# Perceiver layer on one core: queries and keys made by token and turned, the decay's product through the ring

## The reference, cut to what matters

```python
x = x + cross_attention(layernorm(x), ctx)        # 16 heads of 32: q from x, k and v from ctx
x = x + gated_delta_attention(layernorm(x))       # 16 heads of 32, a recurrence over the tokens
x = x + top2_of_8_experts(layernorm(x))

# in the cross attention
q = x @ q_w + q_b;  kv = ctx @ kv_w + kv_b;  softmax(q k / sqrt(32)) v @ proj_w + proj_b
# in the second layer
q, k, v, gate = x @ Wq.T, x @ Wk.T, x @ Wv.T, x @ Wg.T;  beta = sigmoid(x @ Wb.T)
alpha = exp(-exp(A_log) * softplus(x @ Wa.T + dt_bias))      # one number per token and head
q, k normalised by head;  S = a S;  delta = (v - k S) beta;  S += k delta;  y = q S
```

## Time and profile before

| | us |
|---|---|
| median of 3 runs | 3865.71 (3864.11 to 3868.39) |
| the profiled execution | 3867.77 |
| its span in the profile | 3866.0 |
| TensorE busy, matmuls | 3238.1 (84%) |
| TensorE busy, weight loads | 2369.7 (61%) |
| VectorE busy | 2025.7 (52%) |
| ScalarE busy | 1134.9 (29%) |
| GpSimd busy | 988.6 (26%) |
| mean granted TensorE clock | 0.916 |

### The profile page before, as it was taken

One profiled execution on the slowest core, in us unless ns is written; L12 is line 12 of the kernel. 1 busy time (PEld: TensorE's weight loads), 2 busy tenths in 40 slices (PEclk: granted clock), 3 DMA queues, 4 the chain that ended last, 5 costly groups with the idle time before them and its releaser, 6 DMA issues. The chain is left out here.

```text
span 3866.0 us, 102111 instructions
## 1 busy us (share of the span) xinstructions
PE 3238.1 (84%) x42226; PEld 2369.7 (61%) x42226; DVE 2025.7 (52%) x4203; ACT 1134.9 (29%) x2656; POOL 988.6 (26%) x895
## 2 busy tenths in 40 slices
PE   7999999899999899999999899999836656698964
PEld 5777676677676677677767677677624444344521
DVE  2232566666666665566677566666723333580212
ACT  2333333333333333333333333333301111222310
POOL 2222222222222222222232222222123333200123
PEclk9999999999999999999999999999957666798987
DMA  4222322222222222222222322222173433234467
GB/s 157 83 67 67 101 73 69 93 94 71 69 89 80 77 88 76 77 92 87 71 74 70 102 73 72 84 96 71 54 215 100 113 97 102 94 121 119 138 215 234
DMA packets 297925, 379.11 MB, mean 98 GB/s; under 512 B 159568, under 2 KB 212304, under 8 KB 296016
## 3 DMA queue, kind: packets, MB, share of 16 engines
q1 hardware_dynamic: 287184, 338.19, 27.6%
q0 software_dynamic: 10240, 33.56, 2.5%
HBM read 258.17 MB, written 189.01 MB: 116 GB/s over the span
## 5 line engine op out<-in xcount | busy, mean ns | idle before, releaser
L117 PE MATMUL ring<-cond_high,wkv_high 128*128 128x342 f32 (+1 forms) x1152 | 406.0, 352 | 47.0 <-issue 24.6
L117 PE MATMUL ring<-cond_low,wkv_high 128*128 128x342 f32 (+1 forms) x1152 | 368.9, 320 | 0.0
L117 PE MATMUL ring<-cond_high,wkv_low 128*128 128x342 f32 (+1 forms) x1152 | 368.9, 320 | 0.0
L593 ACT ACTIVATE k_t<-ring,kvb 128x342 f32<-128x342 f32 (+1 forms) x384 | 209.4, 545 | 521.3 <-PE ring L117 521.0
L662 ACT ACTIVATE prob<-score,neg_max 128x257 f32<-128x257 f32 x512 | 235.9, 474 | 313.1 <-DVE neg_max L782 313.1
L117 PE MATMUL ring<-wkv_high,cond_high 128*128 128x512 f32 x768 | 320.1, 417 | 0.0
L117 PE MATMUL mix<-experts,xs_t 128*128 x624 | 309.8, 644 | 0.0
L170 DVE TENSOR_TENSOR prod<-prod 128x256 f32<-128x256 f32 (+5 forms) x352 | 302.4, 859 | 12.1
L166 DVE TENSOR_TENSOR prod<-coef,deltas 128x64 f32<-128x64 f32 (+30 forms) x248 | 304.0, 1226 | 5.0
L117 PE MATMUL ring<-wkv_low,cond_high 128*128 128x512 f32 x768 | 304.2, 396 | 0.0
L117 PE MATMUL ring<-wkv_high,cond_low 128*128 128x512 f32 x768 | 303.3, 395 | 0.0
(11 more groups left out here) (199 smaller groups left out, 6014.8 us busy)
## 6 DMA issues: line engine op xcount, KB each, us to landing
cond<-cond_t_dram SPq DMA_DIRECT2D x128, 385.5 KB, 4.2
xs<-slot_rows SPq DMA_DIRECT2D x78, 256.0 KB
slot_rows<-ys SPq DMA_DIRECT2D x78, 256.0 KB
x_rows<-x SPq DMA_DIRECT2D x64, 256.0 KB, 3.1
vb_rows<-vgb SPq DMA_DIRECT2D x64, 256.0 KB, 3.2
x_in<-x_dram SPq DMA_DIRECT2D x32, 256.0 KB, 4.7
v_last_s<-v_last_rows SPq DMA_DIRECT2D x512, 0.5 KB
kk_rows<-kk_rows_s SPq DMA_DIRECT2D x32, 256.0 KB, 2.7
```

Of the source, the lines that this page charges most:

```text
L117: last = pe.matmul(out, lhs_t, rhs, start=(i == 0), stop=(i == len(terms) - 1))
L593: act.activation(k_t[:, group, at:at + n], ring_bank[bank][:, 0:n], ACT.Identity, bias=kvb[:, group:group + 1]).then_inc(ring.free[bank], 1)
```

## The change

Queries and keys of both layers (KK, QQ, QT) are made token by channel with `by_token` (new ring jobs KR1, QR1, QR), moved by ScalarE back over the rows they came from (`x1n`, `x1n`, `xn`), and then turned by four transposes each into the ring jobs KK, QQ and QT, whose readers stay as they were. The decay's product becomes a ring job AL, read by VectorE out of its bank, and stands before KR1. QQ is turned after LD; the wait for `grams_read` stands before QT's transposes, after QR. The ring's order changes accordingly. `by_channel` is gone.

```diff
--- before.py
+++ after.py
@@ -45,12 +45,12 @@
 class Ring:
 
 
-    A = ["K00", "K01", "K02", "K03", "K10", "K11", "K12", "K13", "XT", "K20", "K21", "K22", "K23", "QT",
+    A = ["K00", "K01", "K02", "K03", "K10", "K11", "K12", "K13", "XT", "K20", "K21", "K22", "QR", "K23", "QT",
          "V00", "V01", "L0", "O0", "V10", "V11", "L1", "O1", "V20", "V21", "L2", "O2", "V30", "V31", "L3",
          "O3", "PR"]
-    BOTH = ["K00", "K01", "K02", "K03", "K10", "X1T", "K11", "K12", "KK", "QQ", "K13", "XT", "LD", "K20", "K21",
-            "BT", "GT", "K22", "K23", "QT", "V2", "V00", "V01"] + A[16:]
-    B = ["X1T", "KK", "QQ", "LD", "BT", "GT", "V2"]
+    BOTH = ["K00", "K01", "K02", "K03", "K10", "X1T", "K11", "K12", "AL", "KR1", "K13", "KK", "QR1", "XT", "LD", "QQ",
+            "K20", "K21", "BT", "GT", "K22", "QR", "K23", "QT", "V2", "V00", "V01"] + A[17:]
+    B = ["X1T", "AL", "KR1", "KK", "QR1", "LD", "QQ", "BT", "GT", "V2"]
 
     def __init__(self, full, free):
         self.full, self.free = full, free
@@ -361,8 +361,6 @@
         def by_group(per_head):
             return per_head.rearrange("p (g a) t -> p a g t", a=4)
 
-        alpha_columns = score[:, 0, D - H:D]
-
         ring = Ring([sem("ring0_full"), sem("ring1_full")], [sem("ring0_free"), sem("ring1_free")])
         attn_loaded = sem("attn_loaded")
         cond_loaded = [sem("cond0_loaded"), sem("cond1_loaded")]
@@ -376,7 +374,7 @@
         exp_done, prob_ready = sem("exp_done"), sem("prob_ready")
         turned_ready, prob_t0_ready, prob_t1_ready = sem("turned_ready"), sem("prob_t0_ready"), sem("prob_t1_ready")
         kq_ready = sem("kq_ready")
-        alpha_ready, minus_abs_ready, log_ready = sem("alpha_ready"), sem("minus_abs_ready"), sem("log_ready")
+        minus_abs_ready, log_ready = sem("minus_abs_ready"), sem("log_ready")
         steps_ready, decay_masked = sem("steps_ready"), sem("decay_masked")
         grams_ready, squares_ready, norm_ready = sem("grams_ready"), sem("squares_ready"), sem("norm_ready")
         kk_ready, grams_read = sem("kk_ready"), sem("grams_read")
@@ -631,16 +629,20 @@
                     move_keys(u, 1, 2)
                 if b_:
                     softplus_log(u)
-                    move_kq(u, 0, "KK")
-                    move_kq(u, 1, "QQ")
+                    move("KR1", u, x1n[:])
                 if a:
                     move_keys(u, 1, 3)
+                if b_:
+                    move_kq(u, 0, "KK")
+                    move("QR1", u, x1n[:])
+                if a:
                     move("XT", u, xn_t[:].rearrange("p c t -> p (c t)"))
                 if b_:
                     wait_stored(qk_stored, u)
                     bank = ring.wait_full(act, "LD", u)
                     act.activation(decay[:].rearrange("p h t -> p (h t)"), ring_bank[bank][:], ACT.Exp)\
                         .then_inc(ring.free[bank], 1)
+                    move_kq(u, 1, "QQ")
                 if a:
                     move_keys(u, 2, 0)
                     move_keys(u, 2, 1)
@@ -651,6 +653,7 @@
                     sigmoid("GT", u, steps_of[:].rearrange("p h t -> p (h t)"), copy=vgb[:, 1, :]).then_inc(silu_ready, 1)
                 if a:
                     move_keys(u, 2, 2)
+                    move("QR", u, xn[:])
                     move_keys(u, 2, 3)
                 if b_:
                     move("V2", u, vgb[:, 0, :])
@@ -701,8 +704,9 @@
                     dve.wait_ge(steps_done, group * N + t + 1)
 
             def log_decays(u):
-                dve.wait_ge(alpha_ready, u)
-                own.then(dve.tensor_tensor(z[:], alpha_columns, dtb[:], ALU.add))
+                bank = ring.wait_full(dve, "AL", u)
+                dve.tensor_tensor(z[:], ring_bank[bank][:, 0:H], dtb[:], ALU.add).then_inc(ring.free[bank], 1)
+                ring.wait_read(dve, "AL", u)
                 dve.scalar_tensor_tensor(minus_abs[:], z[:], -1.0, z[:], ALU.mult, ALU.min).then_inc(minus_abs_ready, 1)
 
             def spread_decays(u):
@@ -822,7 +826,7 @@
             turn(0)
             for u in range(1, LAG):
                 turn(u)
-            before, per_group = own.n, GU * 16 + 3 * (N - 1) + sum(len(folds(t)) for t in range(N))
+            before, per_group = own.n, GU * 15 + 3 * (N - 1) + sum(len(folds(t)) for t in range(N))
             with dve.Fori(0, NG - 2) as group:
                 own.turn(before, group, per_group)
                 for quarter in range(GU):
@@ -864,14 +868,6 @@
                 bank, full = bank_of(name, u)
                 for c in range(DC):
                     last = pe.transpose(bank[:, c * P:c * P + P], row[:, c * P:c * P + P], ident[:])
-                last.then_inc(full, 1)
-
-            def by_channel(name, u, weights, rows_t):
-
-                bank, full = bank_of(name, u)
-                for g in range(HG):
-                    w = slice(g * P, g * P + P)
-                    last = products(pe, bank[:, w], [(weights[:, c, w], rows_t[:, c, :]) for c in range(DC)])
                 last.then_inc(full, 1)
 
             def by_token(name, u, rows_t, weights):
@@ -947,11 +943,16 @@
                     keys(u, 1, 2)
                 if b_:
                     ring.wait_read(pe, "X1T", u)
-                    products(pe, alpha_columns, [(x1n_t[:, c, :], wa[:, c, :]) for c in range(DC)]).then_inc(alpha_ready, 1)
-                    by_channel("KK", u, wattn[:, 1], x1n_t)
-                    by_channel("QQ", u, wattn[:, 0], x1n_t)
+                    bank, full = bank_of("AL", u)
+                    products(pe, bank[:, 0:H], [(x1n_t[:, c, :], wa[:, c, :]) for c in range(DC)]).then_inc(full, 1)
+                    by_token("KR1", u, x1n_t, wattn[:, 1])
                 if a:
                     keys(u, 1, 3)
+                if b_:
+                    ring.wait_read(pe, "KR1", u)
+                    turn_rows("KK", u, x1n)
+                    by_token("QR1", u, x1n_t, wattn[:, 0])
+                if a:
                     pe.wait_ge(xn_ready, u + 1)
                     turn_rows("XT", u, xn)
                 if b_:
@@ -959,6 +960,8 @@
                     bank, full = bank_of("LD", u)
                     pe.matmul(bank[:], later[:].rearrange("p b s -> p (b s)"), steps_of[:].rearrange("p h t -> p (h t)"),
                               start=True, stop=True).then_inc(full, 1)
+                    ring.wait_read(pe, "QR1", u)
+                    turn_rows("QQ", u, x1n)
                 if a:
                     keys(u, 2, 0)
                 if b_:
@@ -974,11 +977,13 @@
                     by_token("GT", u, x1n_t, wattn[:, 3])
                 if a:
                     keys(u, 2, 2)
+                    ring.wait_read(pe, "XT", u)
+                    by_token("QR", u, xn_t, wq)
                     keys(u, 2, 3)
-                    ring.wait_read(pe, "XT", u)
+                    ring.wait_read(pe, "QR", u)
                     if b_:
                         pe.wait_ge(grams_read, u)
-                    by_channel("QT", u, wq, xn_t)
+                    turn_rows("QT", u, xn)
                 if b_:
                     bank, full = bank_of("V2", u)
                     for c in range(DC):
```

## The result

The changed kernel takes 3949.17 us (median of 4 runs, 3945.03 to 3953.05) against 3864.91 us before (4 runs): ratio 1.0217, 95% interval 1.0199 to 1.0235. It is slower, as forecast, but by 84 us where 38 were forecast, and it lies above the range.

The account below looks back on a forecast made before the run. TensorE was taken as busiest, racing VectorE's chain to `prob`. Extra work per sort of turn summed to 37.8 us on the profiled 3867.77, giving 3905.6, or 3903.5 us as median; range 3880 to 3928 with the ring-starving rival.

Parts of the forecast that it names:

- The product with 512 moving columns: On TensorE, four 128-column passes take 465 ns against 446 ns for one of 512, so only 4% is gained.
- The decay's product in the ring is free: K13 must wait for VectorE's reading: 4.07 us in the worst turn, covered by 4.38 us of AL and KR1.
- The two new ring waits: TensorE waits for ScalarE's bank readings: 0.2 us at QR1 after KK, 0.3 us at K20 after QQ.
- V2's wait for K23's reading: V2, now after four short transposes, waits another 0.2 us for its bank.
- Sum up to the grams: +1.4: Extra TensorE time per turn before the grams: 2 x 0.45 for KK and QQ, plus ring waits of 0.2 and 0.3.
- QT is ready at about the same time, +0.05: From grams to `q_s`, QT's extra 0.34 us is offset by a vanished 0.35 us wait for ScalarE.
- Fourth quarters pay 0.1: In every fourth turn VectorE already comes 1.5 to 1.6 us late, so the shift fits: 0.1 us each.
- By sorts of turn: Turns 1 to 4 lack time steps; later ones are quarters of a group, differing in whether VectorE waits for grams and QT.
- The wait for `prob` in the fourth quarters: TensorE's wait for VectorE's probabilities there shrinks from 4.9 to some 3.2 us; clock drops after it were let stand.
- the weight loads, of which there are a quarter as many, were hidden well enough: In KK, QQ and QT, fewer weight loads gain nothing; the long form gains only 4%.
- a rival in which the clock falls: Three short jobs and waits, some 3 us, lower the clock at K20: 43 us more, 3947 us; chance 0.06.
- That the chain through VectorE decides, turn by turn: Extra TensorE work counts only where VectorE waits for it: 1.45, 1.4, 1.45 and 0.1 us by quarter.

Follow-up runs that it names:

- the changed kernel with 29 pads: Changed kernel with 29 tiny 32 x 32 matmuls run once ahead of TensorE's loop, moving later instructions 116 places: 3925.39 us, ratio 1.0163.
- both kernels at their best places: Program shifted by tiny matmuls ahead of the loop: changed kernel by 140 places, 3899.93 us; kernel before by 24 places, 3855.65 us.
- Six pads in the kernel before: Kernel before with 6 tiny matmuls run once ahead of the loop, a shift of 24 places: 3855.65 us, ratio 0.9987.
- 9 pads: Kernel before shifted by 36 places with tiny matmuls run once ahead of the loop: 3912.18 us, ratio 1.0137.

## Why the prediction was wrong

**What held.** The product with 512 moving columns is hardly faster than that with 128: QR 3.67 us in the changed kernel, V2 118.3 us in 32 turns, 3.70 each, at full clock. The rule of 131 against 81 ns in the Trainium skill ("TensorE: Matmul & The Clock Gate", "Back-to-back issue gap") gives no gain here. The direction followed from that. The decay's product in the ring is free; z came 4.1 us after it in turn 17, with K13 due at 4.3; in two turns it came after 4.4 and 4.7, and the waits for `z` sum to 0.6 us in the run. The two new ring waits were forecast at 0.2 and 0.3 us and are 0.20 and 0.25 (7.7 us in 31 turns for K20). V2's wait for K23's reading was forecast at 0.2 and is 0.20.

**What was mis-sized.** "Sum up to the grams: +1.4" measured 1.59. I divided busy times by counts. Busy times of successive groups overlap at their ends, by 0.14 us a product here; from start to start KK and QQ took 7.15 us for two, 3.58 each and not 3.72 (1478.54 in the earlier trace rows to the start of K13 at 1485.69). "QT is ready at about the same time, +0.05" measured +0.37: the 0.35 us of a weight load's wait on ScalarE in the earlier trace rows was no time of the matmuls, which started on time; taking it away gave nothing back. "Fourth quarters pay 0.1" measured 0.7 in the changed kernel with 29 pads, 89.38 against 88.65 us a turn: the shift had to fit into 1.5 us of lateness and, at 1.59 and 0.37, no longer did. With both kernels at their best places the change costs 3899.93 - 3855.65 = 44 us, with both idle times at 1 us 63 us; 38 were forecast. By sorts of turn, the changed kernel with 29 pads, whose idle time is that of the kernel before, is longer than it by these us, worked out from the two traces:

```
            turns 1-4   first   second   third   fourth quarters
forecast       1.65      1.45     1.4     1.45      0.1
measured       2.66      2.11     2.36    1.61      0.73
```

These terms sum to 58 us over the 31 turns of the traces against 37 forecast. They alone would have left the result at the top of my range (3925 us as measured). The clock is not their cause: it is low for 96 us of the loop there, against 139 us in the kernel before. The wait for `prob` in the fourth quarters, forecast at 3.2 us, is 3.84 us in the changed kernel without pads and with 29.

**What failed.** Of the miss of 46 us about half is the sum above, 63 us for the change's own work instead of 38. The other half was in no term: the step "the weight loads, of which there are a quarter as many, were hidden well enough", by which fewer instructions cost and gave nothing. Their absence moved the border in the stream, from the 147th to the 205th record, 116 places. The code gives nearly that: 80 instructions fewer ahead of the grams in a turn (KK and QQ) and 40 fewer in turn 0, ahead of the loop (QT). With it the stop in the grams went from 1.0 to 2.0 us, and in 16 turns the clock fell behind it. Putting the border back returned 24 us of 84, moving it on to its best place another 25. The idle time stood in the waits of the kernel before (30.5 us, "issue"), and I took it for a property of the grams that the change doesn't touch. I had a rival in which the clock falls, at K20 and for lack of work in short transposes, and gave it 0.06 and 3947 us. The time was nearly that, but not the mechanism: no version with the three short jobs in a row shows a drop that begins in them, so nothing here bears out the rule that I had named for it, that of the Trainium skill on transposes ("TensorE: Matmul & The Clock Gate", "Part 4: PE-mode transpose").

**What nobody forecast.** By sorts of turn, changed against before, us:

```
            turns 1-4   first   second   third   fourth quarters
before        82.3      86.8     86.7     85.3     88.7
changed       85.3      91.6     86.5     88.3     90.5
```

The second quarters cost nothing: their wait for `prob` fell from 3.8 to 0.50 us and the clock stayed up there, the transposes running in 1.09 us. Changed kernel, turn 17 (a first quarter), then turn 18 (a second):

```profile
1567.16 1.97 PE L891 MATMUL turned<-ident,prob 128*128 128x128 f32 x8 [3.73 <-DVE prob L793]
...
1655.62 1.09 PE L891 MATMUL turned<-ident,prob 128*128 128x128 f32 x8 [0.50 <-DVE prob L793]
```

The first quarters pay most, 4.8 us: there VectorE waits for both the grams and QT, so that the stop, the slow BT and the change's own work all reach `prob`. That the chain through VectorE decides, turn by turn, was right; it also hides part of a gain. Six pads in the kernel before took 23 us out of the grams and 4 us off the median. In the traces turns 1 to 4 and the first to third quarters became shorter by 25 us in sum, and the six fourth quarters longer by 1.6 us each, all of it behind their first transposes, with a wait for `prob` of 4.95 us instead of 4.55 and the clock low for 6.7 us behind it instead of 5.7.

## What to carry to other kernels

An idle time with no releaser at a fixed instruction of a loop, in a run of very small matmuls, depends on where the program lies: before a change is judged, and before two versions are compared, shift the loop by some tens of instructions and look whether that idle time moves. Here the same work spans 3856 to 4064 us by that alone, more than the change's own cost of 44 to 63 us. A price taken as busy time over count is too high for short groups; take starts to starts, and don't credit a weight load's wait that no matmul shows.

## What was unexpected of the hardware

The 256 matmuls of 32 x 32 blocks, with their loads, stop once a turn in most versions, for 0.2 to 2.6 us, at places that move by one instruction for each instruction put ahead of the loop; the fetch packet precedes the restart by 2.4 to 2.6 us on the mean of each version with such a stop in 20 turns or more. Stops of 2.0 us on the mean were followed by the lower clock in 16 to 27 of 31 turns, stops of 1.5 us in BT (9 pads) in 3, and stops of 1.0 us in none. The stop behind the loop's branch moved too, from 4.0 to 7.3 us between PR and K00 on the mean, and why it is shortest in the changed kernel was not tried out. That the fetch itself is the cause rests on the packets and on the moves of the place; no run changed the fetch alone.
